# Twelve of sixteen couples masked on VectorE instead of eight, in a four-layer graph network

## The reference

```python
# layer 0: one head of graph attention
H = X @ W;  e = leaky_relu(s[:, :, None] + t[:, None, :])      # s, t: H times half of a
relu(softmax(e + where(A > 0, 0, -1e9)) @ H)
# layer 1: eight heads of 16, the same with masking by adj, then elu
# layer 2: the relations 1 to 7 of adj (a 0/1 matrix has only relation 1)
agg = ((adj == 1) / degree) @ x @ rel_weights[1] + x @ self_w.T + self_b
relu(layernorm(agg) * gamma + beta)
# layer 3: four heads of 32
Wh = einsum('bsf,hfd->bhsd', features, W)
scores = einsum('bhsd,bhtd->bhst', Wh, Wh) / sqrt(32)
scores = where(adj > 0, scores, NEG_INF)
softmax(scores) @ Wh
```

## Time and profile before

| | us |
|---|---|
| median of 3 runs | 2438.4 |
| lowest, highest | 2432.07, 2440.47 |
| the profiled execution | 2435.11 |
| its span, first to last instruction | 2433.3 |

### The profile page before, as it was taken

One profiled execution on the slowest core, in us unless ns is written; L12 is line 12 of the kernel. 1 busy time (PEld: TensorE's weight loads), 2 busy tenths in 40 slices (PEclk: granted clock), 3 DMA queues, 4 the chain that ended last, 5 costly groups with the idle time before them and its releaser, 6 DMA issues.

```text
span 2433.3 us, 56856 instructions
## 1 busy us (share of the span) xinstructions
PE 2226.6 (92%) x23701; PEld 1498.8 (62%) x23701; DVE 1986.4 (82%) x4206; ACT 1946.5 (80%) x2166; POOL 180.4 (7%) x134
## 2 busy tenths in 40 slices
PE   6668999999999999999999999999999999998876
PEld 5667576575856657585665757566585765658431
DVE  4677788889888888988889888888988878897666
ACT  3958698887889878788987879898787988878734
POOL 0000000010000001000000100001010000100010
PEclk8879999999999999999999999999999999999989
DMA  4552061523315253341524324143432415301000
GB/s 92 140 114 71 5 145 53 121 75 92 82 47 132 59 113 80 76 92 45 131 71 105 88 54 114 44 123 79 105 89 45 114 53 123 80 27 48 24 18 18
DMA packets 190865, 193.77 MB, mean 80 GB/s; under 512 B 129368, under 2 KB 165328, under 8 KB 187728
## 3 DMA queue, kind: packets, MB, share of 16 engines
q1 hardware_dynamic: 183008, 132.99, 20.0%
q0 software_dynamic: 7600, 57.15, 12.0%
HBM read 151.26 MB, written 40.43 MB: 79 GB/s over the span
## 4 chain that ended last, share of the span: by engine, by line
PE 68%; ACT 11%; issue 6%; DVE 6%; DMA 2%; POOL 0%; SPq 0%; POOLq 0%; ACTq 0%; DVEq 0%
PE kp L1146 12%; PE fp L1020 10%; PE kp L1129 9%; PE fp L945 8%; PE kp L1001 7%; ACT weight L1376 5%; PE kp L1122 4%; PE kp L1070 4%; DMA shared<-shared 2%; PE kp L1067 2%; ACT ramp L1328 1%; PE fp L1038 1%; PE fp L869 1%; PE kp L1086 1%; PE kp L1163 1%
## 5 line engine op out<-in xcount | busy, mean ns | idle before, releaser
L1328 ACT ACTIVATE ramp<-s1row,tbig 128x1024 fp8e4<-128x1024 f32 x854 | 909.3, 1148 | 11.9 <-DVE weight L1672 11.9
L1376 ACT ACTIVATE weight<-kp,shift 128x1024 f32<-128x1024 f32 x480 | 511.2, 1111 | 206.4 <-PE kp L1129 188.3
L1146 PE MATMUL kp<-weight,w 128*33 128x512 f32 x1920 | 456.8, 599 | 17.9 <-DVE weight L1818 6.6
L1672 DVE TENSOR_TENSOR weight<-ramp,AT 128x512 int32<-128x512 int32 x512 | 343.3, 689 | 153.7 <-PE fp L1020 98.7
L1020 PEld LDWEIGHTS fp<-vh_parts,weight 128*128 128x128 fp8e4 x8192 | 389.9, 97 | 83.7 <-DVE weight L1672 41.2
L1020 PE MATMUL fp<-vh_parts,weight 128*128 128x102 bf16 x8192 | 417.6, 208 | 21.0 <-DVE weight L1672 15.5
L1818 DVE SCALAR_TENSOR_TENSOR weight<-AT,weight 128x1024 f32<-128x1024 fp8e4 x272 | 321.5, 1219 | 37.6 <-ACT weight L1376 37.3
L1129 PE MATMUL kp<-shared 32*128 32x512 f32 x1920 | 274.7, 641 | 13.8 <-ACT weight L1376 13.7
L1146 PEld LDWEIGHTS kp<-weight,w 128*33 128x33 f32 x1920 | 94.4, 110 | 312.7 <-issue 224.0
L945 PEld LDWEIGHTS fp<-features,weight 128*128 128x128 f32 x1840 | 207.9, 192 | 28.7 <-issue 27.0
L945 PE MATMUL fp<-features,weight 128*128 128x129 f32 x1840 | 213.4, 276 | 5.0 <-DVE weight L1578 4.9
(11 more groups left out here) (251 smaller groups left out, 2715.9 us busy)
## 6 DMA issues: line engine op xcount, KB each, us to landing
s1row<-s_rows_dram SPq DMA_DIRECT2D x128, 512.0 KB, 4.1
adj_bf_dram<-in_adj_dram POOLq DMA_DIRECT2D x15, 2048.0 KB, 13.3
AT<-turned POOLq DMA_DIRECT2D x15, 1024.0 KB, 7.5
x<-in_x_dram SPq DMA_DIRECT2D x16, 512.0 KB, 4.4
out_dram<-elu SPq DMA_DIRECT2D x16, 512.0 KB, 3.2
xfT<-s_row_dram SPq DMA_DIRECT2D x15, 512.0 KB, 4.6
shared<-shared SPq DMA_DIRECT2D x30, 256.0 KB, 3.5
elu<-x POOLq DMA_DIRECT2D x15, 512.0 KB, 4.7
```

Of the source, the lines that this page charges most:

```text
L1146: last = pe.matmul(kp[side(h), 0, :], values3(b)[:, (2 * J + x) * H3 + h, :], weight3[:, w % P_RING, x * HALF:(x + 1) * HALF], start=(J == ...
L1328: act.activation(ramp[:, u % R_RING, :], s1row[:, h % S_RING, :] if b or h else kp_pair, ACT.Relu, bias=tbig1[:, jt, h:h + 1], scale=BIG, ...
L1376: act.activation(weight3[:, w % P_RING, :], score_banks(b, w).rearrange("p a n -> p (a n)"), ACT.Exp, bias=shifts3(b)[:, h:h + 1], scale=R ...
L1672: dve.tensor_tensor(edge_words[:, u % B_RING:u % B_RING + 2, :], ramp_words[:, u % R_RING:u % R_RING + 2, :], AT_words[:, third, jt:jt + 2 ...
```

## The change

`MASKED` grows from eight couples to twelve: 2, 7, 9 and 15 are new. For these, in every batch but the last, TensorE no longer makes the mask product, and VectorE masks the exponentials. All tables of the order hold new numbers. One wait is new on SyncE, since in the first batch the row of head 0 is now loaded last of the three.

```diff
-    MASKED = (4, 6, 8, 10, 11, 12, 13, 14)
+    MASKED = (2, 4, 6, 7, 8, 9, 10, 11, 12, 13, 14, 15)
...
-            (dict(adjacency=0, far=5, out=10, sources=[2, 3, 4, 7, 9], sources_ahead=[12, 13, 14], spread_row=8,
-                 store_row=6, store_sources=11, x=1),),
+            (dict(adjacency=0, far=8, out=10, sources=[3, 2, 5, 4, 6], sources_ahead=[12, 14, 13], spread_row=9,
+                 store_row=7, store_sources=11, x=1),),
...
                 elif edges_ready.any_before(b):
                     sp.wait_ge(edges_ready.sem, edges_ready.before(b))
+                if b == 0 and h == S_RING:
+                    sp.wait_ge(s1_loaded[0].sem, s1_loaded[0].of(0))
                 sp.dma_start(s1row[:, h % S_RING, :], s1_dram[h:h + 1].broadcast_to([P, N])) \
                     .then_inc(s1_loaded[h].sem, 16)
```

More of the change, by code:

```diff
@@ new lines, in graph_stack @@
+            (dict(affine2=-1, columns1=[68, 69], cut1=[70, 72], cut1_third=[74, 75], divide1=62, elu1=64, finish0=53,
+                 finish1=61, finish3=-1, head1=[8, 13, 21, 28, 38, 44, 55, 60], lengths3=-1, low2=73, masked3=[-1, -1,
+                 -1, -1, -1, -1, -1, -1, -1, -1, -1, -1, -1, -1, -1, -1], maxima1=65, maxima3=-1, maximum0=22,
+                 most0=17, norm0=59, norm1=67, norm3=-1, out2=-1, ramps=[-1, -1, -1, -1, -1, 5, -1, -1, -1, -1, 12,
+                 -1, -1, -1, -1, 19, -1, -1, -1, -1, 32, -1, -1, -1, -1, 41, -1, -1, -1, 51, -1, -1], relu2=-1,
+                 rest2=71, shift0=29, shift3=-1, shifts1=66, stats2=-1, stats3=-1, tail3=-1, top0=15, top1=63,
+                 unit0=[31, 33, 36, 37, 43, 46, 48, 49], unit1=[0, 1, 2, 3, 4, 6, 7, 9, 10, 11, 14, 16, 18, 20, 23,
+                 25, 26, 27, 30, 34, 35, 39, 40, 42, 45, 47, 50, 52, 54, 56, 57, 58], z0=24),),
@@ new lines, in graph_stack @@
+            (dict(affine2=18, columns1=[83, 85], cut1=[89, 91], cut1_third=[93, 94], divide1=66, elu1=76, finish0=72,
+                 finish1=63, finish3=-1, head1=[8, 14, 21, 27, 34, 44, 52, 59], lengths3=38, low2=92, masked3=[-1, -1,
+                 50, -1, 58, -1, 69, 71, 73, 75, 78, 80, 82, 84, 87, 88], maxima1=79, maxima3=40, maximum0=39,
+                 most0=29, norm0=74, norm1=86, norm3=28, out2=10, ramps=[-1, -1, -1, -1, 2, -1, -1, -1, 7, -1, -1, -1,
+                 -1, -1, -1, -1, -1, -1, -1, -1, -1, 33, -1, -1, 43, -1, -1, 47, -1, -1, -1, -1], relu2=23, rest2=90,
+                 shift0=51, shift3=42, shifts1=81, stats2=13, stats3=-1, tail3=-1, top0=26, top1=77, unit0=[60, 61,
+                 62, 64, 65, 67, 68, 70], unit1=[0, 1, 3, 4, 5, 6, 9, 11, 12, 15, 16, 17, 19, 20, 22, 24, 25, 30, 31,
+                 32, 35, 36, 37, 41, 45, 46, 48, 49, 53, 55, 56, 57], z0=54),),
@@ L675, in graph_stack @@
[L675 to L677 removed]
+            (dict(adjacency=2, far=-1, out=-1, sources=[1, 3, 6, 7, 8], sources_ahead=[10, 12, 11], spread_row=5,
+                 store_row=4, store_sources=9, x=0),),
+            (dict(adjacency=2, far=9, out=-1, sources=[1, 3, 5, 4, 8], sources_ahead=[11, 13, 12], spread_row=7,
+                 store_row=6, store_sources=10, x=0),),
```

216 lines of the change are left out of this document (98 added, 118 removed).

## The result

| | us |
|---|---|
| before, median of 4 runs | 2437.3 (2432.07 to 2440.47) |
| after, median of 4 runs | 2523.6 (2520.38 to 2527.65) |
| ratio, 95% interval | 1.0357 (1.0341 to 1.0374) |

What follows compares the result with a forecast made beforehand. TensorE was taken to bound the edge-product stretch, with VectorE also full around layer 0's weights. Per period +3.7 - 2.8 - 2.0 = -1.1 us, over 14 intervals -15, gave 2420, forecast as 2423 us; range 2385 to 2452.

Steps and rivals of the forecast that it cites:

- That is 2.8 us: Edge-product stretch: TensorE loses one couple's mask products (0.9 us) and one couple's values (1.84), moved behind the first layer-0 weight.
- stretch I: Part of a period with the edge products, 81.27 us; TensorE busy 76.68, VectorE 64.78; TensorE said to bound it.
- II: Part of a period with layer 0's weights, 30.06 us; VectorE busy 29.01, TensorE 29.25, both called full.
- I take 2.0: TensorE's idle time at layer 3's start: 2.0 us a period recovered by the new order, bounds nothing and 3.2.
- Sums +3.7: Layer 2's sums on TensorE start 3.7 us later a period, bounds 2.2 and 5.6.
- 5.6: VectorE reaches the end of L1732 5.6 us later: 6.8 of added masks less 1.24 of covered wait.
- the slack of 1.9 us: Before the change, L1732 ends 1.9 us before TensorE begins layer 2's sums; subtracted from the delay.
- The wait for st: VectorE's 1.24 us wait for ScalarE's st, while layer 1 is prepared, is covered by a mask placed ahead.
- VectorE decides: Slower rival, 18%: path from first layer-0 weight to L1732 adds 1.5 us a period, 2459; far end 2566.
- stretches II and III together grow by more than about 4.8: Growth in us, on TensorE's side too, of layer-0 weights plus layer-1 preparation, beyond which the slower rival decides.
- The marks that I gave for "slow": Signs of a slow outcome: waits for L1818 before L1146 growing from 97.4 us, or ScalarE waiting on s1row.
- at 0, with 10 us either way: Warm-up and the part behind 2260 us: new orders there counted at 0, with 10 us either way.

Runs made afterwards that it cites:

- old_order_couple2: Kernel before with its old orders, couple 2 alone also masked on VectorE, its step added in stretch I: 2445.5 us, ratio 1.0033.
- seam_mended: New order up to the first layer-0 weight, before's behind; first layer-3 copy and couple 4's values behind two weights, maxima earlier: 2448.8 us, ratio 1.0045.
- early_scores: Changed kernel; a masked couple's second wait for exponentials moved from ahead of both units' scores to between them: 2499.8 us, ratio 1.0253.

## Why the prediction was wrong

- **The sum's base failed, not its prices.** L1818's price (1219 ns), 240 mask products, 120 masks: right. But the sum treated the new orders as the old ones with items moved, and took that an engine has only its work and the named waits. The orders by themselves cost 101 us, some 70 at full clock.
- **"That is 2.8 us", stretch I.** (0.9 + 1.84 is 2.7.) The 0.9 of mask products is mostly waiting time filled (old_order_couple2: 0.1 to 0.2 us a period). The 1.84 of values is moved, not removed: I took it from I and did not add it in II, where I had read both engines as full. seam_mended measures it: 1.9 less in I, 2.0 more in II. In the changed kernel the same piece grows by 2.5, which VectorE's added couple would do alone; the two can't be told apart there.
- **"I take 2.0" of idle recovered.** The reverse: the waits at layer 3's start went from 0.40, 1.43 and 1.33 us to 0.28, 2.35 (qdiag) and 1.15, and the clock behind them costs 2.0 a period. From the sums to the first weight it is 81.5 us instead of 81.7, and 79.5 at full clock; the forecast's terms make it 76.9.
- **Sums +3.7.** Measured +7.0: 5.4 at full clock (30.5 + 36.5 against 61.6), 1.6 of clock. At full clock the mechanism is the forecast one and its size is off: L1734 ends 66.95 us behind the first weight, L1732 before 59.72, so 7.2 later and not 5.6; less the slack of 1.9 us that is 5.3, and TensorE indeed waits 0.56 for L1734. The wait for st is gone in these periods, as forecast (its 1.74 is there when scores 10 and values 8 run at the lower clock). What the 5.6 lacks is the wait of 1.50 for TensorE's turned maxima, which the new order puts behind scores 12. That VectorE's added masks alone set this path isn't shown: with before's masks it is as long, and early_scores takes 1.2 us off it without touching VectorE's work; nor do the runs clear them, since VectorE is busy 5.1 us more on a path that is 5.4 longer.
- **The clock** stood in no term and in no rival, though the prediction names a wait before masked scores. Filling the waits brought back 31 us.
- **The rival "VectorE decides"** had the place (from first weight to L1732, scores 9 and 10 side by side) and the mechanism of the masked couple, but priced it at +1.5 a period (measured +6.4) and called it VectorE's. Its mark, "stretches II and III together grow by more than about 4.8", is met: 7.0. But it is no proof of the masks: with before's masks the path is as long. The marks that I gave for "slow" did not show it: the waits for L1818 stayed at 97.4 us in all. L1131's wait for exponentials, 14 to 75 us, would have.
- **Warm-up and end, "at 0, with 10 us either way"**: -2.5 and +5.9, within it.

What stays open: how much of the orders' 70 us is the serial couple (24 with its clock), the seam of values or the single placements, and why the clock falls at the third place in some periods and not in others, which moves kernels here by up to some 14 us. Of the moves made by hand, earlier maxima and earlier scores brought 23 and 24 us, the others lost; none came at the price of the step moved.

## What to carry to other kernels

Work that an engine does between two waits may cost nothing, and its removal gives nothing: look at what it would wait for next before pricing it. Price a newly searched order as a whole: list per stretch what left it *and* what arrived, and look for pairs of steps that hand a buffer back and forth with nothing between them. Where TensorE gets a new wait of 2 us, price the slower matmuls behind it as well, which here cost more than the wait.
